# Attention sums as two halves of 64 rows in both sums banks, the gate product in a ring slot, the queries' rows turned by VectorE

## The reference, cut to what matters

```python
q = (query @ Wq.T).reshape(B, L, H, D) * scale            # 16 heads of 16
k = (key @ Wk.T).reshape(B, -1, H, D)
v = (value @ Wv.T).reshape(B, -1, H, D)
scores = sigmoid(einsum('blhd,bshd->bhls', q, k))         # no softmax: every score by itself
o = einsum('bhls,bshd->blhd', scores, v).reshape(B, L, E)
x = x + (o @ Wo.T)                                        # query = layernorm(x)
# FFN on n = layernorm(x): gate logits n @ gate_w.T, softmax over 16 experts,
# each expert takes its 128 best rows of a batch of 512*2/16 = 64, gelu(g) * u, Wd, weighted, added;
# and for all rows gelu(n @ Ws_g.T) * (n @ Ws_u.T) @ Ws_d.T; x = x + both
```

## Time and profile before

| what | value |
|---|---|
| median of 2 runs | 1304.04 us (1303.62 to 1304.46) |
| the profiled execution's own time | 1303.73 us |
| its span | 1301.9 us |
| granted TensorE clock, mean | 0.999 |
| TensorE, weight loads, VectorE, ScalarE, GpSimd busy | 1281.9, 760.7, 756.8, 984.5, 285.0 us |
| sigmoids (L883) | 789.6 us |
| score matmuls (L1774) | 312.5 us |
| sums matmuls (L1803), both banks | 210.5 + 205.9 us |

### The profile page before, as it was taken

How to read it: one execution, slowest core, us unless ns; L and a number is a source line. 1 busy time by engine, 2 the same in 40 slices (tenths; PEclk the granted TensorE clock), 3 DMA queues, 4 the chain that set the end, 5 groups by cost and what they waited for, 6 DMA issues and landing times.

```text
span 1301.9 us, 25111 instructions
## 1 busy us (share of the span) xinstructions
PE 1281.9 (98%) x9976; PEld 760.7 (58%) x9976; DVE 756.8 (58%) x1433; ACT 984.5 (76%) x1148; POOL 285.0 (22%) x288
## 2 busy tenths in 40 slices
PE   8999999999999999999999999999999999999997
PEld 6445445444444444444444453336888888888887
DVE  6564484375366438537535632215558778888883
ACT  5888988999998898998999989996232355555553
POOL 2000030020003003002000200500000567777645
PEclk9999999999999999999999999999999999999999
DMA  7785973874766586387467638713533577777854
GB/s 210 185 188 123 143 176 115 126 152 144 131 137 161 124 140 159 119 133 140 156 124 140 138 88 133 194 38 114 195 130 103 180 201 191 192 191 193 194 111 49
DMA packets 118724, 190.79 MB, mean 147 GB/s; under 512 B 22448, under 2 KB 71600, under 8 KB 118608
## 3 DMA queue, kind: packets, MB, share of 16 engines
q1 hardware_dynamic: 98768, 155.21, 51.7%
q0 software_dynamic: 19648, 33.72, 12.4%
q10 hardware_dynamic: 192, 0.26, 0.1%
HBM read 108.43 MB, written 55.61 MB: 126 GB/s over the span
## 4 chain that ended last, share of the span: by engine, by line
PE 87%; issue 5%; DVE 3%; DMA 2%; ACT 1%; POOL 1%; POOLq 0%; SPq 0%; DVEq 0%; ACTq 0%
PE score L1862 19%; PE score L1774 18%; PE acc L1803 14%; PE misc L1803 13%; PE score L1603 5%; PE score L1589 5%; PE score L1889 3%; PE score L1880 2%; PE score L1612 2%; ACT probs L883 1%; PE score L1884 1%; PE acc L1880 1%; PE misc L1880 1%; PE score L1642 1%; PE score L1630 1%
## 5 line engine op out<-in xcount | busy, mean ns | idle before, releaser
L883 ACT ACTIVATE probs<-score 128x1024 f32<-128x1024 f32 (+1 forms) x832 | 789.6, 1026 | 77.4 <-PE score L1774 70.8
L1774 PE MATMUL score<-queries,keys 48*128 48x512 f32 (+1 forms) x1664 | 312.5, 438 | 6.4 <-ACT probs L883 4.2
L1774 PEld LDWEIGHTS score<-queries,keys 48*128 48x128 f32 (+1 forms) x1664 | 139.3, 180 | 274.9 <-ACT probs L883 211.6
L1803 PE MATMUL acc<-probs,values 128*32 128x512 f32 (+1 forms) x1664 | 210.5, 601 | 0.0
L1803 PE MATMUL misc<-probs,values 128*32 128x512 f32 (+1 forms) x1664 | 205.9, 600 | 0.0
L1037 DVE TENSOR_REDUCE whole<-score 128x512 f32<-128x1024 f32 (+1 forms) x75 | 77.0, 1026 | 196.6 <-PE score L1589 119.7
L736 POOL DMA_DIRECT2D ctx_raw<-ctx_t x32 | 23.4, 733 | 645.0 <-DVE ctx_lo L1015 564.6
L808 POOL DMA_INDIRECT gathered<-norm_scr,gather_row x64 | 80.7, 1261 | 225.9 <-DVE gather_row L1395 210.7
L898 ACT ACTIVATE gelu<-score 128x512 f32<-128x512 f32 (+1 forms) x97 | 54.7, 581 | 83.8 <-PE score L1862 83.7
L1862 PE MATMUL score<-tok_hi,gu_hi 128*128 128x512 f32 (+1 forms) x388 | 117.1, 383 | 0.0
L821 POOL DMA_INDIRECT out<-result,add_row x64 | 106.7, 1668 | 47.3 <-DVE result L1384 25.4
(11 more groups left out here) (267 smaller groups left out, 1568.5 us busy)
## 6 DMA issues: line engine op xcount, KB each, us to landing
keys<-key_scr SPq DMA_DIRECT2D x180, 200.2 KB, 8.1
key_scr<-key_parts SPq DMA_DIRECT2D x45, 512.0 KB, 8.3
gu_raw<-w_gu SPq DMA_DIRECT2D x17, 1024.0 KB
ctx_raw<-ctx_t POOLq DMA_DIRECT2D x24, 512.0 KB, 5.3
queries<-query_parts SPq DMA_DIRECT2D x186, 64.0 KB, 2.3
d_raw<-w_d SPq DMA_DIRECT2D x17, 512.0 KB
norm<-xn SPq DMA_DIRECT2D x224, 32.0 KB
xn<-x SPq DMA_DIRECT2D x8, 512.0 KB, 3.8
```

The lines of the kernel that those rows point to most:

```text
L883: act.activation(probs[0:rows, (n + 1) % RING, 2 * pair:2 * pair + 2, :], score[SLOT[k]][0:rows, :, :], ACT.Sigmoid, scale=SCALE).then_inc ...
L1774: mm = pe.matmul(score[SLOT[k]][0:rows, g, :], keys[quarter % KEY_RING][of, pair, P * st:P * st + rows], queries[half][of, e, pair, :], st ...
L1803: mm = pe.matmul(sums_bank[n // NST % 2][32 * c:32 * (c + 1), :], values[b % 2][0:rows, st, half, c, :], probs[0:rows, (n + 1) % RING, c, ...
```

## The change

The diff does these things. `weighted_sum` makes each head's sum as two matmuls, one over rows 0 to 63 into `acc` and one over rows 64 to 127 into `misc`, in every quarter; so its first tile waits for `acc_out` of the quarter just before. `acc_out` reads both banks, one after the other. The gate product of batches 0 to 6 goes into a ring slot. The T steps are gone but for batch 0's first: x of the next batch, normalised, is transposed in blocks by VectorE at quad 20 (`turn_x`, into `resid`, which is free then), placed by 16 DMAs of GpSimd (`place_x`), and split at quad 32 (`split_x`); `split_norm` moves to quad 47. The reloads of `resid` and `xn` and the store of the turned norm move on SyncE's queue, the context loads on GpSimd's. The three strings are new: they have 278 runs of W, and in 19 of the 31 changes of quarter the last W of one quarter and the first W of the next stand side by side (before the change, in 3). In the FFN's first units VectorE's steps, one gate product and the rounds of `choose` stand in another order.

```diff
-                ("T", c, 0), ("T", c, 1), ("Q", c, 0), ("K", c, 0, 2)]
+                ("K", c, 0, 2), ("K", c, 1, 2), ("V", c, 2, 0), ("Q", c, 0)]
...
-EACH = ("SSWWSSTSWSSSWWSTSTSSWWSSTSSWSSSWWSSTSSWSSSWWSSTSWSSSWWSTSTSSWWSSSWWSSSWWSSTSWSSTSWSSSWWSTS"
-        "WSSSWWSSSWWSTSWSSTSWSSTSWSSSWTWSSTSWSSTSWSSTSWSSSWWSTTSSWSTSWSSSWWSSSWWSSTSWSSSWWSSSWWSS")
+OPENING = ("SSTSSWSSTWSSTSWSSTSWSSTSWSSSWWSTSWSSSWWSTSWSSTSWSSTSWSSTSWSSSWWSSWSTSTSSWWSSSWWSSWSTSTSSWW"
+           "SSTSWSSTSWSSSWWSTSTSSWWSSSWWSSTSSWSSSWWSSTSWSSTSWSSSWWSTTSTSWSSSWWSSSWWSSTSWSSSWWSSSWWSS")
+
+EACH = ("SWWSSSWWSSTSWSSTSWSSTSWSSTSTSSWWSSTSWSSSWWSSSWWSSTSWSSSWWSSSWWSSTSWSSSWWSSSWWSSTSWSSTSWSSS"
+        "WWSSSWWSSTSWSSTSWSSSWWSSTSTSSWTSSSWWSSSWWSSTSWSSSWWSTTSSWSSWSTSWSSTSWSSSWWSSSWWSSSWWSS")
...
-           "WSSSWWSSSWWSSSWTSSWSTSSWSSSWWSSSWWSSTSSWSSSWWSSSWWSSSWWSSSWWSSTSSWSSTSWSSSWWWW")
+           "WSSSWWSSSWWSSSWWSSSWWSSSWTSTSSWSSWSTSSWSSWSSWSTSSWSSSWWSSSWWSSTSSWSSSWWSSSWWWW")
...
-           [s for s in STEPS[b] if s[0] == "S" or (s[0] == "T" and s[1][0] != "G")]]
+           [s for s in STEPS[b] if s[0] in "ST"]]
...
             def load_resid_a(b):
-                if b:
-                    sp.wait_ge(post_stored, STORE * b)
+                if b + 1 < B:
+                    sp.wait_ge(x_placed, PLACE_DMAS * (b + 1))
                 else:
-                    sp.wait_ge(direct_written, 16 * len(DIRECT))
-                    sp.wait_ge(first_keys_in[2], STACK_DMAS)
+                    sp.wait_ge(resid_stored, 16 * b)
                 sp.dma_start(resid[:], x_rows[b]).then_inc(x_again_in, 16)
...
-                sp.wait_ge(misc_copied, COUNT["T", b - 1, KC - 1])
+                if b > 1:
+                    sp.wait_ge(x_split, b - 1)
+                else:
+                    sp.wait_ge(misc_copied, COUNT["T", 0, KC - 1])
...
-                    if what == "S" and which == 2 * QPB // 2:
-                        load_resid_a(0)
...
                         if q == 0:
                             stack_queries(b, 1)
                             stack_keys(4 * b + 2)
+                            if b >= 2:
+                                store_norm_t(b - 2)
...
-                        if q == 24:
+                        if q == 24 and b + 1 == B:
                             store_norm_t(b - 1)
                             load_resid_a(b)
...
@@ -660,6 +666,9 @@
                         if task == ("K", b + 1, 1, NCH - 1):
                             stack_keys(4 * b + 4)
                             stack_keys(4 * b + 5)
+                            load_resid_a(b)
+                            if b + 2 < B:
+                                load_x(b + 2)
...
+                pool.wait_ge(x_turned, b)
+                for i in range(BLOCKS):
+                    for j in range(BLOCKS):
+                        pool.dma_start(x_raw[TURN * j:TURN * (j + 1), :, P * i:P * (i + 1)],
+                                       x_blocks[TURN * i:TURN * (i + 1), j::BLOCKS, :]).then_inc(x_placed, 16)
+
+            for kc in range(NCH - 1):
+                load_ctx(1, kc)
             for b in range(1, B):
-                for kc in range(NCH):
-                    load_ctx(b, kc)
+                load_ctx(b, NCH - 1)
                 if b >= 2:
                     place_norm(b - 2)
+                place_x(b)
+                if b + 1 < B:
+                    for kc in range(NCH - 1):
+                        load_ctx(b + 1, kc)
...
             def acc_out(quarter):
                 _, half, e, _ = quad_of(NST * quarter)
-                bank = sums_bank[quarter % 2]
                 dve.wait_ge(quad_done, NST * (quarter + 1))
                 if e == 0:
                     wait_past(dve, o_split, quarter // 2)
-                    dve.tensor_scalar(o_sum[:], bank[:], mine[:, 0:1], None, ALU.mult
-                                      ).then_inc(acc_copied, 1)
+                    dve.tensor_scalar(o_sum[:], sums_bank[0][:], mine[:, 0:1], None, ALU.mult
+                                      ).then_inc(split_step, s.up())
+                else:
+                    dve.wait_ge(acc_copied, quarter)
+                    dve.scalar_tensor_tensor(out=o_sum[:], in0=sums_bank[0][:], scalar=mine[:, 1:2], in1=o_sum[:],
+                                             op0=ALU.mult, op1=ALU.add).then_inc(split_step, s.up())
+                dve.wait_ge(split_step, s.now())
+                dve.scalar_tensor_tensor(out=o_sum[:], in0=sums_bank[1][:], scalar=mine[:, e:e + 1], in1=o_sum[:],
+                                         op0=ALU.mult, op1=ALU.add).then_inc(acc_copied, 1)
+                if e == 0:
                     return
-                dve.wait_ge(acc_copied, quarter)
-                dve.scalar_tensor_tensor(out=o_sum[:], in0=bank[:], scalar=mine[:, 1:2], in1=o_sum[:],
-                                         op0=ALU.mult, op1=ALU.add).then_inc(acc_copied, 1)
...
+            def turn_x(b):
+                dve.wait_ge(xn_ready, b + 1)
+                if b == 1:
+                    dve.wait_ge(direct_written, 16 * len(DIRECT))
+                    dve.wait_ge(first_keys_in[2], STACK_DMAS)
+                else:
+                    dve.wait_ge(resid_stored, 16 * (b - 1))
+                dve.transpose(x_blocks.rearrange("p j (t q) -> p t j q", q=TURN),
...
+            def split_x(b):
+                wait_past(dve, norm_placed, PLACE_DMAS * (b - 1))
+                dve.wait_ge(x_placed, PLACE_DMAS * b)
+                for k in range(KC):
...
+                    dve.tensor_copy(hi, raw).then_inc(split_step, s.up())
+                    dve.wait_ge(split_step, s.now())
+                    last = dve.tensor_tensor(lo, raw, hi.bitcast(F32), ALU.subtract)
+                last.then_inc(x_split, 1)
...
-                if b and q == 22:
+                if b and q == (47 if b + 1 < B else 22):
                     split_norm(b - 1)
...
+                if b + 1 < B and q == (22 if b == 0 else 20):
+                    turn_x(b + 1)
+                if b + 1 < B and q == 32:
+                    split_x(b + 1)
...
             hidden_lo(0, 0, (0, 1))
             hidden_products(0, (2, 3))
             copy_out(AFTER[1])
+            hidden_lo(0, 0, (2, 3))
             second_sums(B - 1)
-            hidden_lo(0, 0, (2, 3))
             norm_scale()
             norm_apply(norm, resid, norm_ready)
 
-            hidden_quarters(1, 1, (0, 1))
+            hidden_products(1, (0, 1))
+            copy_out(AFTER[2])
+            hidden_lo(1, 1, (0, 1))
             shared_result(0)
-            copy_out(AFTER[2])
             hidden_products(1, (2,))
             copy_out(AFTER[3])
...
-                hidden_quarters(n, par, (0, 1))
+                hidden_products(n, (0,))
                 if n == 2:
                     gate_logits(B - 1)
+                hidden_products(n, (1,))
+                if n == 5:
+                    choose(range(4, 5))
+                hidden_lo(n, par, (0, 1))
...
-                    choose(range(4 * (n - 4), 4 * (n - 3)))
+                    choose(range(4) if n == 4 else range(5, CAP // 8))
...
-                        mm = pe.matmul(misc[TURN * t:TURN * (t + 1), 0:P], gate[:, k, :], tokens[:, t, :, :],
+                        mm = pe.matmul(bank[TURN * t:TURN * (t + 1), 0:P], gate[:, k, :], tokens[:, t, :, :],
...
+                    if b:
+                        pe.wait_ge(x_split, b)
                     mm = query_halves(task[2], bank)
...
                 else:
-                    if b + 1 < B:
-                        pe.wait_ge(acc_copied, 4 * (b + 1) + 2)
-                    else:
+                    if b + 1 == B:
                         pe.wait_ge(misc_copied, COUNT[task] - 1)
-                    mm = gate_product(b)
+                    mm = gate_product(b, bank[:, 0, :] if b + 1 < B else misc)
...
-                    wait_past(pe, acc_copied, n // NST - 1)
-                    if n // NST < 2:
+                    wait_past(pe, acc_copied, n // NST)
+                    if n // NST == 0:
...
-                    if n // NST % 4 == 3 and b:
-                        pe.wait_ge(misc_copied, COUNT["G", b - 1])
...
                 for c in range(4):
-                    mm = pe.matmul(sums_bank[n // NST % 2][32 * c:32 * (c + 1), :], values[b % 2][0:rows, st, half, c, :],
-                                   probs[0:rows, (n + 1) % RING, c, :], start=(st == 0), stop=(st == NST - 1))
+                    for part, of in ((0, slice(0, ROWS)), (1, slice(ROWS, rows))):
+                        mm = pe.matmul(sums_bank[part][32 * c:32 * (c + 1), :], values[b % 2][of, st, half, c, :],
+                                       probs[of, (n + 1) % RING, c, :], start=(st == 0), stop=(st == NST - 1))
                 mm.then_inc(quad_done, 1)
...
-                up(n, par, 0, (0, 1))
+                up(n, par, 0, (0,))
                 if n == 2:
                     product(AFTER[4])
```

(21 more changed lines are left out.)

51 lines of the change are left out of this document (21 added, 30 removed).

## The result

The changed kernel takes 1751.4 us (median of 2 runs, 1748.95 to 1753.85), 1.3424 times the 1304.04 before, with an interval of 1.3401 to 1.3448. The forecast was 1335, range 1290 to 1360: the direction was right, the size off by 416 us.

The account below looks back on a forecast made before the run. TensorE was taken as the bound (98% busy, working 839 of attention's 869 us), ScalarE second. Terms 4.0 + 36.1 + 4.0 + 6.0 + 0.1 + 1.4 - 3.5 - 1.6 - 15 = +31.5 on 1303.7 gave 1335 us, range 1290 to 1360.

Parts of the forecast that it names:

- the streaming of the halves: Attention sums: eight 64 x 32 tiles run side by side like four before, adding only stagger, 4.0 us (0 to 7.8).
- stagger of the tiles: Sums runs in attention: four more tiles start 28 ns later per run, 278 runs; 4.0 us taken, ends 0 and 7.8.
- stalls, with VectorE's backlog: Quarter changes: TensorE waits for both copies, 36.1 + 4.0 us; VectorE late at six batches' first change, 6.0 us.
- waits for ScalarE given back: Attention: ScalarE gets ahead while TensorE stalls, so part of TensorE's 30 us of waits goes; 15 us gained, ends 0 and 30.
- T steps and gate: Attention: 14 T leave TensorE, 3.5 us gained; gate product in a slot adds two shape changes seven times, 1.4 us lost.
- FFN order: FFN start: new order shortens two TensorE stalls, of 0.9 and 0.7 us; 1.6 us gained, ends 0 and 2.5.
- The 19 side-by-side stalls: Quarter changes with no step between the sums steps: TensorE waits for VectorE's second copy, 1.9 us each, 36.1 us.
- the changes with two or three S between: Four quarter changes whose score steps hide part of the stall: 2 x 1.1 + 2 x 0.9 = 4.0 us.
- Elsewhere VectorE is idle at the change: Beyond the first quarter change of batches 1 to 6, VectorE was taken to have no backlog at quarter changes.
- A, shape changes cheap: Every S to W to S: weights load across shapes while rows stay 64, 97 us of TensorE work go; 1248 us, 9%.
- B, tiles not at once: Sums: the two halves of a column group follow each other, W takes three passes, 179 us more; 1513 us, 12%.
- C, x late: Next batch's transposed x lands 3 us late seven times, 21 us, with VectorE and TensorE's Q standing; 1355 us, 13%.

Follow-up runs that it names:

- padded kernel: Changed kernel with the second half of each quarter's 13th tile padded with zeros to 64 rows: 1377.2 us, ratio 1.0497.
- experiment 1: The run that gave the padded kernel: changed kernel, second half of the 13th tile padded to 64 rows; 1377.2 us, ratio 1.0497.
- experiment 5: Changed kernel with 32 rows (one real, 31 of zeros) in the second half of the 13th tile: 1740.2 us, ratio 1.331.
- experiment 6: Changed kernel with 33 rows (one real, 32 of zeros) in the second half of the 13th tile: 1394.4 us, ratio 1.0665.
- experiment 10: Changed kernel with 32 rows in the 13th tile's second half, and its four 64-row matmuls ahead of the four 32-row ones: 1427.2 us, ratio 1.0934.
- experiment 7: Changed kernel with the sums of the kernel before (whole tiles, banks in turn, one copy a quarter), all else changed: 1301.3 us, ratio 0.9958.
- experiment 9: Padded kernel with eight extra, thrown-away score matmuls before the wait at each of the 19 side-by-side changes of quarter: 1365.3 us, ratio 1.0472.
- experiment 8: Padded kernel with the two or three following score steps put between the sums steps at the 19 side-by-side changes of quarter: 1354.6 us, ratio 1.0371.
- experiment 12: Experiment 7's kernel, but a quarter's first sums step waits for the copy of the quarter just before: 1333.0 us, ratio 1.0227.

## Why the prediction was wrong, step by step

**The failed step: the streaming of the halves.** "Each W becomes 8 tiles of 64 x 32" is true of 12 tiles in 13. The rows to see it stood there: the records of the last W in a quarter are 65*32, and the new slice leaves the 65th row alone. The forecast's term for the streaming of all tiles was 4.0 us, and it held nothing for the thirteenth. That tile costs 323 - 19 = 304 us (changed against padded kernel). At full clock alone it would be 32 x 6.8 = 217 (7.3 us where eight equal tiles take 0.5), half of the 447 by which the kernel is slower; the other 87 are half clock within the step. Experiments 1, 5 and 6 show it.

**The clock** was a number of the profile before (0.999) that the forecast carried over unasked. Beside those 87 it costs some 70 us of attention outside the thirteenth tiles (374 - 304), and 4 at the FFN's start. That the thirteenth tiles bring it down is shown by experiment 1, in which it falls in none of them; which of "one tile at a time" and "few rows" matters is only partly told apart (experiments 6 and 10).

**With the thirteenth tile mended, the sum by terms** (padded kernel against experiment 7, same order of steps, both in the profiled execution):

| term | forecast | measured |
|---|---|---|
| stagger of the tiles | 4.0 | 416 x 0.027 - 118 x 0.026 = 8.1 |
| stalls, with VectorE's backlog | 36.1 + 4.0 + 6.0 = 46.1 | 59.8 - 11.6 = 48.2 |
| waits for ScalarE given back | -15 | 0 |
| T steps and gate | -3.5 + 1.4 | +0.3 (experiment 7 against before; 1.2 of it a wait of the last kind below) |
| FFN order | -1.6 | -1.7 (same) |
| low clock | none | +12 (for the 24 us taken away in experiment 9; up to 5 more for the other 10) |
| waits that no semaphore ended, outside the stalls | none | 6.3 - 1.2 = +5 |

These sum to 72, and the spans differ by 1374.2 - 1301.9 = 72; that is closer than the clock's term is known. The 19 side-by-side stalls were right, 1.9 us each, and their place too. That the whole row is right to 2 us is partly luck, for two errors cancel. VectorE's backlog was 0.5 us six times, not 1.0: here the norm's sums, of 1.40, delay the first copy, and TensorE stands 2.26 (waits in brackets):

```profile
179.46 1.40 DVE L1121 BATCH_NORM_STATS2 bn<-xn 128x6 f32<-128x256 f32 x4
180.78 0.74 DVE L1164 TENSOR_SCALAR o_sum<-acc,mine 128x512 f32<-128x512 f32 x1
181.55 0.75 DVE L1171 SCALAR_TENSOR_TENSOR o_sum<-misc,mine,o_sum 128x512 f32<-128x512 f32 x1
```

```profile
179.60 0.59 PE L1835 MATMUL misc<-probs,values 64*32 64x512 f32 x1
182.45 0.59 PE L1835 MATMUL acc<-probs,values 64*32 64x512 f32 x1 [2.26 <-DVE o_sum L1171]
...
183.47 1.33 PE L1807 MATMUL score<-queries,keys 48*128 48x512 f32 x6
184.73 1.06 PE L1835 MATMUL acc<-probs,values 64*32 64x512 f32 x1
```

The last of these S, and the W behind it, are already at half clock: the starts behind 183.47 stretch.

Against that, the changes with two or three S between cost 6.5 us and not 4.0. "Elsewhere VectorE is idle at the change" was wrong at batch 0's second change, where it splits the context rows before it copies, and TensorE stands 3.05 us before its W at 93.40:

```profile
90.08 1.22 DVE L1038 TENSOR_TENSOR ctx_lo<-ctx_raw,ctx_hi 128x1024 fp32r<-128x1024 f32 x1
91.69 0.74 DVE L1168 SCALAR_TENSOR_TENSOR o_sum<-acc,mine,o_sum 128x512 f32<-128x512 f32 x1
```

**A term that was not there:** the 30 us read as waits for ScalarE were no reserve. The 211.6 us of the earlier trace rows are those of weight loads; of TensorE's own waits in the kernel before, the list has this:

```profile
PE score L1774 <- ACT probs L883: 4.2, 9, 0.5
```

From S to S it is 0.33 us on average before (402 times) and in the padded kernel (414) alike; the sum over priced steps was 30 short, and I took the rest for waits. With 0 in that place the forecast's sum is 1350.

**The last row of the table** is in the list of TensorE's waits, columns total, times, longest; "issue" means that nothing visible released it:

```profile
PE acc L1835 <- issue: 7.7, 5, 2.1
...
PE score L1666 <- issue: 2.2, 1, 2.2
...
PE score L1646 <- issue: 1.1, 2, 0.8
PE misc L1835 <- issue: 0.5, 1, 0.5
```

That is 11.5 us in 9 places. Three of them, 5.2 us, stand at side-by-side changes of quarter (626.1, 747.9 and 867.1) and last 1.69 to 1.75 us, like those of their kind that the copy ends (1.75 to 1.79): they are stalls, and counted as such. It leaves 6.3 us in six places, against 1.2 in one in experiment 7. The padded kernel has 3328 more matmul records, and the queue that carries instructions moved 1.70 MB instead of 1.28. That TensorE ran out of instructions would fit this, but no run isolates it.

**The rivals.** A, shape changes cheap: wrong; S to W 0.32 and W to S 0.52 before and after. B, tiles not at once: wrong for twelve tiles, and its mechanism, passes queued tile by tile, is what the thirteenth does; the price is the 217 us above, and the clock on top. C, x late: TensorE never waits for it.

## What to carry to other kernels

When a tile is cut, write down the shape of every piece, the ragged last one above all, and don't let shapes alternate (1 and 32 rows were one shape here, 33 and 64 another): order pieces by shape, or pad with zeros, which took no time of their own here. When TensorE will stand still or work with few tiles, put the clock into the sum and not only the wait; useful score steps moved into the stall (experiment 8) brought 22.6 us between the medians, more than the 14 that they filled.

## What was unexpected of the hardware

- Alternating 64-row and 1- or 32-row tiles of 32 columns: 0.97 us for each fp32 matmul of 512 columns, where eight of one shape take 0.88 together (padded kernel, from one sums step to the next).
- The granted clock falls with TensorE busy 100% of the time by the profile (4.10 of 4.10 us), if it runs one small tile at a time.
- It can fall behind an empty stretch of 1.7 to 2.3 us: nine stretches of low clock behind 19 such changes in the padded kernel. It need not: behind that kernel's longest wait, 3.05 us, it stayed up. Where the same changes left 0.9 to 1.5 us empty (experiment 12) two of 19 were followed by a fall, and where they left 0.6 to 1.1 (experiment 9) none; the fall at one of these changes came behind a wait of 2.68 us ahead of the filling.
